# A selective scan on one core: LayerNorm statistics of finished tiles moved from VectorE to ScalarE

## The reference, cut to what matters

```python
def _layernorm(x, axis=-1, eps=1e-05):
    m = jnp.mean(x, axis=axis, keepdims=True)
    v = jnp.var(x, axis=axis, keepdims=True)
    return (x - m) / jnp.sqrt(v + eps)

def step(s, inp):                      # the scan, 512 channels x 16 states
    d, u_i, b_i, c_i = inp
    s = s * jnp.exp(d[..., None] * A) + (d * u_i)[..., None] * b_i[:, None, :]
    y = jnp.einsum('bdn,bn->bd', s, c_i)
    return (s, y)
...
    x = x1 + x                          # x1 = _mamba(_rmsnorm(x))
    x3 = _mlp(_rmsnorm(x))              # three linear layers, relu between
    return x + x3
...
x = _layernorm(x + _L0_attn_ref(x, ...), axis=-1)
```

## Time and profile before

| | us |
|---|---|
| median of 3 runs | 2661.59 |
| lowest and highest run | 2648.98, 2671.50 |
| the profiled execution's own time | 2654.74 |
| its span in the trace | 2653.0 |

### The profile page before, as it was taken

The page is one execution under the profiler, slowest core; times in us unless marked ns, Lnnn a source line. Parts: engine busy times, 40 slices in busy tenths (PEclk is TensorE's granted clock), DMA queues, the critical chain, the costliest instruction groups (busy, mean ns, idle before and its releaser), DMA issues. The chain is left out here.

```text
span 2653.0 us, 48629 instructions
## 1 busy us (share of the span) xinstructions
PE 2319.5 (87%) x16861; PEld 1570.4 (59%) x16861; DVE 1938.5 (73%) x4294; ACT 1505.2 (57%) x3353; POOL 1310.0 (49%) x1257
## 2 busy tenths in 40 slices
PE   4868898989898996879999988888977999999797
PEld 2546465656556564557777755655654665566555
DVE  4999999999999999346667646777765445556545
ACT  5667777777877875333333324544554666655522
POOL 1777778787868686343333323544464222221401
PEclk7859999999998997989999988999998999999899
DMA  5444344444443444020000134234303000000100
GB/s 176 149 135 147 130 151 133 148 130 151 131 149 127 152 130 133 21 76 1 1 1 1 18 75 78 53 66 75 56 3 106 16 22 18 18 18 18 50 14 9
DMA packets 138502, 204.64 MB, mean 77 GB/s; under 512 B 24417, under 2 KB 59362, under 8 KB 138130
## 3 DMA queue, kind: packets, MB, share of 16 engines
q1 hardware_dynamic: 136274, 198.64, 26.1%
q0 software_dynamic: 960, 2.62, 0.3%
q10 hardware_dynamic: 1024, 0.26, 0.1%
HBM read 161.29 MB, written 14.68 MB: 66 GB/s over the span
## 5 line engine op out<-in xcount | busy, mean ns | idle before, releaser
L423 POOL TENSOR_TENSOR ma_seen<-ma_state,ma_cs 128x1024 f32<-128x1024 f32 x256 | 603.5, 2361 | 278.2 <-DVE ma_state L1023 264.1
L1023 DVE TENSOR_TENSOR_SCAN ma_state<-ma_decay,ma_last,ma_drive 128x512 f32<-128x512 f32 x512 | 650.6, 1271 | 0.1
L1010 DVE TENSOR_TENSOR ma_drive<-ma_weight,ma_bs 128x512 f32<-128x512 f32 x512 | 357.3, 698 | 40.8 <-ACT ma_weight L857 9.0
L633 PEld LDWEIGHTS ma_acc<-ident,ma_seen 128*128 128x128 f32 x2048 | 257.4, 152 | 155.5 <-POOL ma_seen L423 91.3
L633 PE MATMUL ma_acc<-ident,ma_seen 128*128 128x128 f32 x2048 | 292.2, 293 | 65.1 <-POOL ma_seen L423 64.7
L867 ACT ACTIVATE ma_decay<-ma_dt,ma_a_neg 128x512 f32<-128x512 f32 x512 | 338.4, 710 | 0.1
L2146 DVE CUSTOM_DVE_ANT_0 sw_score<-sw_score,both_band 128x256 f32<-128x256 f32 (+1 forms) x512 | 197.4, 448 | 51.6 <-PE sw_score L1960 40.5
L2084 ACT ACTIVATE sw_prob<-sw_turned 128x512 f32<-128x512 f32 (+1 forms) x256 | 135.5, 581 | 172.0 <-PE sw_turned L1974 148.9
L104 POOL TENSOR_TENSOR moe_h_low<-both_V,light_wqkv 128x512 fp32r<-128x512 f32 x80 | 104.9, 1311 | 247.5 <-DVE light_wqkv L100 240.0
L1882 POOL TENSOR_SCALAR_AFFINE_SELECT sw_prob<-sw_prob 128x512 f32<-128x512 f32 x128 | 84.1, 657 | 206.9 <-ACT sw_prob L2084 206.9
L1606 DVE TENSOR_TENSOR both_V<-both_V,moe_up 128x512 f32<-128x512 f32 x80 | 55.0, 687 | 120.6 <-PE moe_up L1395 75.3
(11 more groups left out here) (555 smaller groups left out, 5588.6 us busy)
## 6 DMA issues: line engine op xcount, KB each, us to landing
ma_bs<-bc_rows SPq DMA_DIRECT2D x256, 256.0 KB, 3.2
ma_cs<-bc_rows SPq DMA_DIRECT2D x256, 256.0 KB, 3.2
ma_h<-kept_taps SPq DMA_DIRECT2D x28, 256.0 KB, 4.3
both_wide<-both_kh SPq DMA_DIRECT2D x28, 192.0 KB, 4.4
both_wide<-both_qh SPq DMA_DIRECT2D x20, 256.0 KB, 4.6
x_rows<-X SPq DMA_DIRECT2D x1, 4096.0 KB
light_rows<-li_y SPq DMA_DIRECT2D x32, 128.0 KB, 1.7
out_dram<-li_o SPq DMA_DIRECT2D x32, 128.0 KB, 1.8
```

Source lines behind the costliest of these rows:

```text
L423: g.tensor_tensor(out=seen[n % RR][:, :, :], in0=state[n % SR][:, :, :], in1=each(cs[n % CR][:, :], 2), op=ALU.mult).then_inc(S["seen_full ...
L633: ins = t.matmul(accs(j, mm), seen[n % RR][:, mm, j * P:(j + 1) * P], K["ident"][:, :], is_transpose=True, start=False, stop=(last_ and j ...
L1010: v.tensor_tensor(out=drive[mm][:, :], in0=weight[mm][:, :], in1=bs[n % CR][:, :], op=ALU.mult).then_inc(S["drive_done"], 1)
L1023: v.tensor_tensor_scan(state[n % SR][:, mm, :], decay[s % DR][:, :], drive[mm][:, :], last[:, k, m:m + 1], ALU.mult, ALU.add).then_inc(S[" ...
```

## The change

The row statistics of groups 0 to 5 leave DVE. In their place:

- POOL turns the four sums into negative means (`away`, one small instruction at q = 24, ahead of `dt_rest`).
- ACT squares the tile with that negative mean as bias and accumulates the row sum of the squares (`powers`, tiles 0 and 1 at q = 29, tiles 2 and 3 at q = 30). The squares themselves go to `xT2`, which is free by then.
- POOL's `finishes` uses these sums and moves from q = 29 to q = 31.
- ACT's `normalized` moves from the end of q = 31 of the same group to q = 5, 6, 7 and 8 of the next one (for group 5, which has no next body, into the tail, behind the first `outputs`).

Groups 6 and 7 keep DVE's statistics, in the tail.

```diff
+        BY_DVE = GROUPS - 2
+            def away(i):
+                pool.wait_ge(S["y_out"], GT * (i + 1))
+                g.tensor_scalar(away3[:, :], total3[:, :], -1.0 / D, 0.0, ALU.mult, ALU.add).then_inc(S["away3_done"], 1)
             def finishes(i):
                 pool.wait_ge(S["var3"], i + 1)
                 since(pool, "x_done", GT * i)
-                g.tensor_scalar(mv[:, :, 1], mv[:, :, 1], 1.0, LN_EPS, ALU.mult, ALU.add).then_inc(S["root_in3"], 1)
-                g.tensor_scalar(shift3[:, :], mv[:, :, 0], -1.0, 0.0, ALU.mult, ALU.add).then_inc(S["root_in3"], 1)
+                if i < BY_DVE:
+                    g.tensor_scalar(mv[:, :, 1], power3[:, :], 1.0 / D, LN_EPS, ALU.mult, ALU.add).then_inc(S["root_in3"], 1)
+                    g.tensor_scalar(shift3[:, :], away3[:, :], 1.0, 0.0, ALU.mult, ALU.add).then_inc(S["root_in3"], 1)
+                else:
...
-                    if q == 29 and two:
+                    if q == 24 and two:
+                        away(i - 2)
+                    if q == 31 and two:
                         finishes(i - 2)
...
             def outputs(i, j):
                 out = filled("out", i, j)
-                a.activation(xg(i, j), out[:, 0:D], ACT.Copy).then_inc(S["y_out"], 1)
+                if i < BY_DVE:
+                    a.activation(xg(i, j), out[:, 0:D], ACT.Copy, accum_out=total3[:, j:j + 1]).then_inc(S["y_out"], 1)
+                else:
+                    a.activation(xg(i, j), out[:, 0:D], ACT.Copy).then_inc(S["y_out"], 1)
+            def powers(i, tiles):
+                act.wait_ge(S["away3_done"], i + 1)
+                act.wait_ge(S["h1_done"], HB * (i + 2))
+                since(act, "rstd3_done", i)
+                for j in tiles:
+                    ins = a.activation(xT2[:, j // 2, j % 2 * D:(j % 2 + 1) * D], xg(i, j), ACT.Square, bias=away3[:, j:j + 1],
+                                       accum_out=power3[:, j:j + 1])
+                if j == GT - 1:
+                    ins.then_inc(S["var3"], 1)
...
-                    if q == Q - 1 and two:
-                        for j in range(GT):
-                            normalized(i - 2, j)
+                    if q in (29, 30) and two:
+                        powers(i - 2, ((0, 1), (2, 3))[q - 29])
+                    if q in (5, 6, 7, 8) and i >= 3:
+                        normalized(i - 3, q - 5)
...
             outputs(LAST - 1, 0)
+            for j in range(GT):
+                normalized(LAST - 2, j)
             for pair in ((0, 1), (2, 3)):
                 for j in pair:
                     turned_back(LAST, j)
...
-                        if two and (q, mm) in ((5, 0), (6, 0), (21, 0), (24, 0)):
-                            statistic(i - 2, (5, 6, 21, 24).index(q))
-                        if two and (q, mm) == (24, 1):
-                            variances(i - 2)
```

More of the change, by code:

```diff
@@ L289, in mamba_phase @@
         rstd3, shift3 = A.sb("rstd3", [P, GT]), A.sb("shift3", [P, GT])
+        total3, away3, power3 = (A.sb(n, [P, GT]) for n in ("total3", "away3", "power3"))
         dbc = xs1[0:48, 0:2, :].rearrange("p j d -> p (j d)")
@@ L308, in mamba_phase @@
             "gated", "back_out", "x1_full", "x1_added", "z_out", "gz_full", "squared2", "rstd2_done", "xs2_full", "xT2_full",
-            "h1_done", "h2_done", "y_out", "var3", "rstd3_done", "shift3_done", "x_done")}
+            "h1_done", "h2_done", "y_out", "away3_done", "var3", "rstd3_done", "shift3_done", "x_done")}
         b_in, c_in = ([A.sem(f"{n}{k}") for k in range(CR)] for n in ("b_in", "c_in"))
@@ L441, in finishes @@
                 since(pool, "x_done", GT * i)
-                g.tensor_scalar(mv[:, :, 1], mv[:, :, 1], 1.0, LN_EPS, ALU.mult, ALU.add).then_inc(S["root_in3"], 1)
-                g.tensor_scalar(shift3[:, :], mv[:, :, 0], -1.0, 0.0, ALU.mult, ALU.add).then_inc(S["root_in3"], 1)
+                if i < BY_DVE:
+                    g.tensor_scalar(mv[:, :, 1], power3[:, :], 1.0 / D, LN_EPS, ALU.mult, ALU.add).then_inc(S["root_in3"], 1)
+                    g.tensor_scalar(shift3[:, :], away3[:, :], 1.0, 0.0, ALU.mult, ALU.add).then_inc(S["root_in3"], 1)
+                else:
+                    g.tensor_scalar(mv[:, :, 1], mv[:, :, 1], 1.0, LN_EPS, ALU.mult, ALU.add).then_inc(S["root_in3"], 1)
+                    g.tensor_scalar(shift3[:, :], mv[:, :, 0], -1.0, 0.0, ALU.mult, ALU.add).then_inc(S["root_in3"], 1)
                 pool.wait_ge(S["root_in3"], 2 * i + 2)
@@ L1051, in variances @@
             def variances(i):
-                dve.wait_ge(S["stat3"], GT * (i + 1))
+                dve.wait_ge(S["stat3"], GT * (i + 1 - BY_DVE))
                 since(dve, "shift3_done", i)
```

## The result

The changed kernel took 2667.49 us (median of 20 runs, 2660.68 to 2687.06), the one before 2658.80 (median of 20 runs, 2648.98 to 2678.91): ratio 1.0043, 95% interval 1.0024 to 1.0061. That is 8.7 us more where 8.9 were worked out, and the 2667 us forecast lies on the median. The median is also moved by how many executions were long ones: 8 of the 20 after are above 2670 us and 3 of the 20 before. The medians of the others are 2664.3 and 2657.3, 7.0 apart, so the whole time shows some 7 to 9 us and no more exactly than that.

The account below looks back on a forecast made before the run. DVE sets the pace, except at group ends, where ACT and PE form a second chain. On-time groups +1.8, late +5.9, group 7 -0.6, tail +1.8 make +8.9 us: 2667 us (middle of 2663.6 and 2670.5), range 2651 to 2683.

Parts of the forecast that it names:

- The place and price of the squares: Four ACT squares between the eviction at q = 29 and the `weight` copies: 0.49 us each, copies 1.96 later.
- seams: First drive of the next group: 1.49 us wait in each of two on-time groups, +2.33 in each of three late ones.
- What DVE saves: Statistics leaving DVE's list: 0.61 us saved per group, 3.7 us over groups 2 to 7.
- The term at q = 15: Middle of a late group: DVE's wait grows by the 0.24 us saved before it.
- late group: Group where PE's clock returns late in the second MLP layer; groups 3, 5, 6 forecast +1.96 us each.
- The tail: Group 5 normalization behind the output copy, ahead of `turned_back`, for which PE's projection waits: +1.8 us.
- The moved instructions, `away`, `finishes`: Normalizing at q = 5 to 8 hidden; `away` nothing, or 0.3 us per group if exposed; `finishes` shows at most 0.2.
- The wait of DVE for a decay at q = 26: Sign against the forecast: DVE waiting for a decay instead of the `weight` copies; no step or size given.
- The clock rivals: PE's clock returns late in every group, 2672 us, chance 0.17; or late in none, 2659 us, chance 0.13.

Follow-up runs that it names:

- e1: Changed kernel with ACT's squares moved from q = 29 and 30 to 27 and 28; scan block ends at 1151.2 us, ratio to before 1.0029.
- e5: Changed kernel with every square of q = 29 and 30 done twice; scan block ends at 1172.4 us, ratio to before 1.0108.
- e3: Changed kernel with squares at q = 27 and 28 and group 5's normalizing behind `turned2`; scan block ends at 1148.5 us, ratio to before 0.9999.
- e4: Changed kernel without squares (constant instead), group 5's normalizing behind `turned2`; scan block ends at 1148.1 us, ratio to before 1.0103.
- e7: e3 with ACT's second-layer eviction moved from q = 29 to 30; scan block ends at 1140.7 us, whole 2653.29 us, ratio to before 0.9988.
- e8: Kernel before with ACT's second-layer eviction moved from q = 29 to 30; scan block ends at 1143.2 us, whole 2654.78 us, ratio to before 0.9991.
- e6: Kernel before with only the normalizing moved to q = 5 to 8 (group 5's behind `turned2`); scan block ends at 1144.6 us, ratio to before 0.9983.
- e2: Changed kernel with group 5's normalizing moved in the tail behind `turned2`; scan block ends at 1151.6 us, ratio to before 1.0036.

## Why the prediction was right

**The place and price of the squares: right, and shown.** 1.96 us was worked out, 1.97 measured. e1 takes the price away by the place alone, e5 doubles it. Summed over the five seams, the marked waits of after are 12.8 us (1.58, 3.23, 1.58, 3.27, 3.15) where those before were about 3.4: 9.4 more, against 2 x 1.49 + 3 x 2.33 = 10.0, nearly the same. Taken from drive to drive, as the forecast was, the seams lost 3.0 before and 12.2 after, 9.1 more; the late ones lost 3.0 to 3.2 and not 3.34, since DVE reaches them later than forecast (q = 26).

**What DVE saves: a right bound, too large as a term.** 3.7 us went into the sum. A group's statistics did take 0.58 out of DVE's list (4.0 against 3.9 at each of three pairs, and the variances), 3.5 in all, but 1.1 came back as waits for the decay at q = 26, so that the list is 2.4 us shorter. That most of it is not gained was right: e3 and e4 end 0.5 and 0.9 us before the kernel before, and without seam waits 1.2 us arrive (e7 against e8).

**The term at q = 15: wrong.** It was put at +0.24 in each late group. The marks in groups 3, 5 and 6 before sum to 2.4; after, in groups 3 to 5 they sum to 1.3 and group 6 has none. The step failed because it took the moment of the clock's return at steps 5 to 8 as given. The same eight matmuls of the output projection took 2.80 us before, at a granted clock of 0.67, and 2.14 after, at 0.88, in group 3 (timeline of PE, before and after):

```profile
465.01 2.80 PE L581 MATMUL ma_bank<-ma_w_out,ma_h 128*128 128x256 f32 x8
```

```profile
466.49 2.14 PE L594 MATMUL ma_bank<-ma_w_out,ma_h 128*128 128x256 f32 x8
```

**The tail: mechanism right, size too small.** 1.81 us of wait as forecast, and some 2 more from PE at its lower clock, which had not been put into the sum; about 1.4 of them stand behind the wait, and are as long in both other kernels that have it. e1 and e5, with the tail unmended, have 75.8 and 75.5 us, the mended ones 72.2 and 73.0: about 3 us for this edit.

In sum: scan +5.8 (7.1 forecast) and tail +3.6 (1.8 forecast) make +9.4 at the mark. The scan's own terms are seams +9.1 (10.0 forecast), q = 15 -1.1 (+0.7) and DVE's list -2.4 (-3.7), with 0.1 in groups 0 and 1. The errors cancel in part, and this is luck.

**The moved instructions, `away`, `finishes`: right, free as far as shown.** e6 shows it for the normalizing ones at steps 5 to 8; for the others it rests on e1, which still has them, and no run takes them out one by one. The wait of DVE for a decay at q = 26 had been named as a sign against the prediction, in place of waits for `weight`; here it came beside them. In the changed kernel it cost nothing, as DVE waits for the copies at the seam in any case.

**The clock rivals.** The count of late groups stayed at four in after, which the forecast had as likeliest. But where it shows in the traces it is between two and five, and the groups differ (2, 4 and 5 in e2, whose list up to the tail is that of after). What the Trainium skill, TensorE: Matmul & The Clock Gate, Part 1, says, that the same kernel finds the change of clock at other matmuls from run to run, agrees with e2. That the count held in after may be chance.

## What to carry to other kernels

An instruction's price is that of the place it is put in: ask what the engine's next awaited product is, and whether a wait stands between. Moving work to an engine with 22% idle time (ACT in group 3 before) cost its full length behind the last wait ahead of a hand-over, and nothing one to two steps earlier, ahead of such waits. What the relieved engine gains reaches only as far as its next hand-over: here q = 26 and q = 15 took back 2.3 of 3.5 us even where no seam waited. Where one execution spreads by more than the edit is worth, read a mark inside the program and count the disturbed stretches before comparing.

## What the runs showed of the hardware

- A BATCH_NORM_STATS2 whose record is 0.40 us lengthens the stream of DVE by 0.12, start to start; why the rest is hidden was not tried.
- An ACT square of 256 columns that accumulates costs 0.40 us from start to start, and 0.49 with a bias from memory, the read of the accumulator included.
- The same 4129 matmuls of the sliding-window block took 414.5 us at a mean granted clock of 0.94 and 438.4 at 0.87, in kernels that don't differ there. What decides between them stays open: after had 8 of 20 runs above 2670 us, before 3 of 20 beside it and 7 of 29 and 6 of 29 beside the experiments, e6 none of 10, e8 3 of 12.
